# Next pair's matrices and merge ahead of a pair's head scaling; out-projection, norms and feed-forward one turn later

## What is computed

```python
# x: [8, 256, 256]; H, DK, DV = 6, 32, 64
q, k, v = (silu(causal_conv4(x @ W.T, w)) for W, w in ...)      # depthwise, 4 taps
beta = sigmoid(x @ Wb.T);  g = -exp(A_log) * softplus(x @ Wa.T + dt_bias)
q = l2norm(q) * DK ** -0.5;  k = l2norm(k)
def step(S, (qt, kt, vt, gt, bt)):                              # per batch and head, over 256 tokens
    S = S * exp(gt)
    S = S + bt * outer(kt, vt - kt @ S)
    return S, qt @ S
o = scan(step, S0=0)
o = o * rsqrt(mean(o * o, -1) + 1e-5) * norm_w * silu(x @ Wg.T) # gating, per head
x = layernorm(x + o @ Wo.T)
xq = ternary_quantize(x, 0.33, 0.5);  w = ternary_quantize(weight, 0.2, 0.6) + rram_variation
x = layernorm(x + xq @ w.T)
```

## Time and profile before

| | |
|---|---|
| median of 3 runs | 350.73 us (350.22 to 351.06) |
| the profiled execution: its time | 353.02 us |
| its span | 351.2 us |
| TensorE matmuls busy | 252.8 us, 72% |
| VectorE busy | 268.5 us, 76% |
| ScalarE busy | 146.8 us, 42% |
| chain that ended last | TensorE 53%, VectorE 22%, issue 18%, ScalarE 5% |

### The profile page before, as it was taken

The page is one execution under the profiler, slowest core; times in us unless marked ns, Lnnn a source line. Parts: engine busy times, 40 slices in busy tenths (PEclk is TensorE's granted clock), DMA queues, the critical chain, the costliest instruction groups (busy, mean ns, idle before and its releaser), DMA issues.

```text
span 351.2 us, 15117 instructions
## 1 busy us (share of the span) xinstructions
PE 252.8 (72%) x6956; PEld 178.0 (51%) x6956; DVE 268.5 (76%) x660; ACT 146.8 (42%) x271; POOL 9.2 (3%) x14
## 2 busy tenths in 40 slices
PE   2978943986479958958699589776928458967571
PEld 1435421666455535756455356665607357755441
DVE  0688999563999995969999887589999960546966
ACT  1497763255463602734636214635423024024031
POOL 2110000001000000010000000100000000000000
PEclk9999976698989985999989955999876757969898
DMA  7900000000000002000001020000010002000101
GB/s 231 359 0 2 3 1 0 4 4 6 4 5 4 0 0 63 6 4 6 6 4 60 0 63 4 4 7 4 4 60 0 2 5 63 6 5 4 60 1 60
DMA packets 8031, 9.82 MB, mean 28 GB/s; under 512 B 1568, under 2 KB 7072, under 8 KB 7968
## 3 DMA queue, kind: packets, MB, share of 16 engines
q1 hardware_dynamic: 6480, 8.39, 7.2%
q10 hardware_dynamic: 1488, 0.47, 0.5%
HBM read 6.76 MB, written 2.10 MB: 25 GB/s over the span
## 4 chain that ended last, share of the span: by engine, by line
PE 53%; DVE 22%; issue 18%; ACT 5%; DMA 1%; DVEq 0%; SPq 0%; ACTq 0%
PE fr L322 15%; PE pj L335 10%; PE pj L350 5%; PE pg L322 5%; PE pc L322 4%; DVE conv_buf L958 4%; PE po L322 3%; PE pc L479 3%; PE po L479 2%; PE pj L509 2%; DMA xt<-x_t 1%; PE pj L367 1%; DVE tok_buf L970 1%; DVE ss L991 1%; DVE stats L1222 1%
## 5 line engine op out<-in xcount | busy, mean ns | idle before, releaser
L335 PE MATMUL pj<-xt,wproj 128*128 128x512 f32 x96 | 53.6, 706 | 8.4 <-DMA xt<-x_t 6.4
L958 DVE SCALAR_TENSOR_TENSOR conv_buf<-raw,wconv,conv_buf 128x512 f32<-128x512 f32 x72 | 53.3, 755 | 4.9 <-ACT conv_buf L663 3.2
L335 PEld LDWEIGHTS pj<-xt,wproj 128*128 128x128 f32 x96 | 20.0, 220 | 31.0 <-issue 24.0
L662 ACT ACTIVATE raw<-pj 128x512 f32<-128x512 f32 x24 | 14.3, 596 | 34.7 <-PE pj L335 34.7
L1088 DVE TENSOR_TENSOR mq<-fr,ad 128x512 f32<-128x512 f32 x12 | 8.3, 692 | 26.5 <-PE fr L322 26.5
L350 PE MATMUL pj<-xt,wproj 128*128 128x512 f32 x48 | 25.1, 664 | 4.6 <-ACT conv_buf L663 4.6
L322 PE MATMUL fr<-x_t,x 32*32 32x16 f32 x768 | 11.5, 209 | 21.6 <-issue 21.6
L322 PEld LDWEIGHTS fr<-x_t,x 32*32 32x32 f32 x768 | 10.9, 151 | 24.3 <-issue 24.3
L322 PE MATMUL fr<-kga,wu 32*32 32x64 f32 x768 | 14.7, 228 | 7.2 <-issue 7.2
L350 PEld LDWEIGHTS pj<-xt,wproj 128*128 128x128 f32 x48 | 10.0, 213 | 16.4 <-issue 8.4
L727 ACT ACTIVATE s_sb<-po 128x192 f32<-128x192 f32 x12 | 4.0, 330 | 32.8 <-PE po L322 32.8
(11 more groups left out here) (181 smaller groups left out, 578.2 us busy)
## 6 DMA issues: line engine op xcount, KB each, us to landing
xt<-x_t SPq DMA_DIRECT2D x1, 1536.0 KB, 11.4
res<-x SPq DMA_DIRECT2D x3, 512.0 KB, 4.1
out<-hid_buf SPq DMA_DIRECT2D x6, 256.0 KB, 2.1
wproj<-w_proj SPq DMA_DIRECT2D x1, 1024.0 KB, 7.4
xt<-x_t SPq DMA_DIRECT2D x1, 512.0 KB, 5.0
kq<-x SPq DMA_DIRECT2D x1, 512.0 KB, 3.8
wout<-w_out SPq DMA_DIRECT2D x1, 384.0 KB, 11.7
cst<-consts ACTq DMA_DIRECT2D x1, 305.5 KB, 11.4
```

The lines of the kernel that those rows point to most:

```text
L335: mm = pe.matmul(pj[:, j % 2, :], wproj[:, t, j * P:(j + 1) * P], xt[:, t, k * TOK:(k + 1) * TOK], start=(t == 0), stop=(t == KT - 1))
L662: act.activation(raw[:, j, :, TAPS - 1:], bank, ACT.Copy)
L958: e = dve.scalar_tensor_tensor(out=conv[:, d, :, :], in0=raw[:, d, :, m:m + T], scalar=wconv[:, j, m:m + 1], in1=conv[:, d, :, :], op0=ALU ...
```

## The change

On VectorE the head work of a pair is split in two: `head_factors` (sums, root) stays ahead of the next pair's `chunk_matrices`, `head_scale` (scaling and transposes) goes behind `inverse_to_rows`, and `gated` goes into the next turn, behind `inverse`, which is now first in the turn. `attention_sum`, `first_norm` and `ternary` of pair k - 1 move behind the first three conv tiles; `transition_sum` is gone. On TensorE each transition block begins with a product of the identity with `ad`, and ScalarE copies the sum out (`transition_out`). `project_out(k - 1)` stands between the transition blocks of turn k and writes `pj`; `gates(k)` are in turn k instead of k - 1, in turn 3 inside the recurrence and into `fr`; `ternary_turned` is at chunk 5, `feed_forward` at chunks 6 and 7. ScalarE's order follows. `ternary` writes into `hid_buf` instead of `tok_buf`, and the token transpose loses a wait. The heads of the last pair are finished inside the last turn, the first half ahead of the feed-forward sums and the second behind them.

```diff
-        pos = view(tok_buf, 0, TT, HID, dt=BF16)
-        xq = view(tok_buf, TT * HID // 2, TT, HID, dt=BF16)
+        pos = view(hid_buf, 0, TT, HID, dt=BF16)
+        xq = view(hid_buf, TT * HID // 2, TT, HID, dt=BF16)
...
+        a_bank = (pj[:, 0, :], pj[:, 1, :])
...
                 if first(k):
                     pe.wait_ge(ffn_ready, 2)
                 after(pe, tile_out, CONV_TILES, k, CONV_TILES)
-                if not first(k):
-                    after(pe, gate_done, 0, k, GATE_TILES)
-                    after(pe, ffn_in, 0, k - 1, 2)
+                if k > 1:
+                    after(pe, ffn_in, 2, k - 2, 2)
                 for n in range(2):
                     pe.matmul(pj[:, n, 0:UH * CH].rearrange("p (u t) -> p u t", t=CH), identb[:, :],
                               negb[:, :].unsqueeze(1).to_broadcast([P, UH, CH]), start=True, stop=False)
...
                 if b == 0:
                     after(pe, kg_done, 1, k, 1)
                     after(pe, at_done, 1, k, 1)
+                    after(pe, decay_in, 1, k, 1)
+                    after(pe, qe_done, 1, k, 1)
+                pe.matmul(fr[:, b, :], cst[:, C_IDENT:C_IDENT + P],
+                          ad[:, :, :, :].rearrange("p c g x -> p (c g x)")[:, b * MB * 64:(b + 1) * MB * 64],
+                          start=True, stop=False, skip_group_check=True)
                 for n in range(b * MB, (b + 1) * MB):
                     i = n - b * MB
                     mm = by_head(fr[:, b, i * 64:(i + 1) * 64], wu[:, n, 0:DK], kga[:, k % 2, n // G3, n % G3, :],
-                                 start=True, stop=True)
+                                 start=False, stop=True, skip_group_check=True)
                 mm.then_inc(mq_mm, 1)
 
             def new_state(k, c):
...
                 merge_second(k)
                 if front:
                     project(k + 1, 5)
-                solved(k, 0)
-                solved(k, 1)
-                if not first(k):
-                    ternary_turned(k - 1)
-                for b in range(2, 5):
+                for b in range(5):
                     solved(k, b)
                 new_state(k, 0)
                 heads_out(k, 0)
                 new_state(k, 1)
                 for b in range(3):
                     transitions(k, b)
-                    if not front and b < 2:
-                        feed_forward(k - 1, b)
+                    if not first(k) and b < 2:
+                        project_out(k - 1, b)
                 for c in range(1, NC):
                     carried_state(k, c)
                     if c < NC - 2:
                         new_state(k, c + 1)
                     heads_out(k, c)
-                    if front and not first(k) and c in (2, 3):
-                        feed_forward(k - 1, c - 2)
+                    if not front and c <= GATE_TILES:
+                        gates(k, c - 1)
+                    if not first(k) and c == NC - 3:
+                        ternary_turned(k - 1)
+                    if not first(k) and c >= NC - 2:
+                        feed_forward(k - 1, c - (NC - 2))
                 if front:
-                    exponents(k + 1)
                     for g in range(G3):
                         chunk_products(k + 1, g)
+                    exponents(k + 1)
                     if not last(k + 1):
                         for j in range(4):
                             project(k + 2, j)
-                    gates(k + 1, 0)
-                    gates(k + 1, 1)
-                    project_out(k, 0)
-                    project_out(k, 1)
-                    gates(k + 1, 2)
+                    for j in range(GATE_TILES):
+                        gates(k, j)
                     merge(k + 1)
                     if not last(k + 1):
                         project(k + 2, 4)
...
                 act.activation(wu[:, b * WB:b * WB + n, :].rearrange("p u x -> p (u x)"), wu_bank[b][:, 0:n * 96],
                                ACT.Copy).then_inc(wu_out, 1)
 
+            def transition_out(k, b):
+                after(act, mq_mm, b + 1, k, 3)
+                act.activation(mq[:, b * MB:(b + 1) * MB, :].rearrange("p u x -> p (u x)"), fr[:, b, :],
+                               ACT.Copy).then_inc(mq_in, 1)
+
             def state_out(k, c):
                 after(act, s_mm, c + 1, k, NC - 1)
                 act.activation(s_sb[:, (c + 1) % 2, :], s_bank[c % 2][:, 0:G3 * DV], ACT.Copy).then_inc(s_done, 1)
...
                     weight_part(1)
                 if front:
                     tile_out_of_psum(k + 1, 4)
-                if not first(k):
-                    normalize(k - 1, 0)
-                if front:
                     tile_out_of_psum(k + 1, 5)
-                solved_out(k, 0)
-                solved_out(k, 1)
-                if not first(k):
-                    ternary_out(k - 1)
-                for b in range(2, 5):
+                for b in range(5):
                     solved_out(k, b)
                 if first(k):
                     weight_part(2)
                 state_out(k, 0)
                 if front:
-                    for j in range(3):
-                        silu(k + 1, j)
+                    silu(k + 1, 0)
+                transition_out(k, 0)
+                if front:
+                    silu(k + 1, 1)
+                transition_out(k, 1)
+                transition_out(k, 2)
+                if front:
+                    silu(k + 1, 2)
                 for c in range(1, NC):
                     if c < NC - 1:
                         state_out(k, c)
                     if c % 2:
                         heads_out(k, c // 2)
-                    if not front:
-                        if c % 2:
+                        if not front:
                             heads_square(k, c // 2)
-                        continue
-                    if c == 1:
+                    if not front and c <= GATE_TILES:
+                        gate_silu(k, c - 1)
+                    if not first(k) and c == 3:
+                        normalize(k - 1, 0)
+                    if front and c == 4:
                         square(k + 1)
-                    if 3 <= c < 6:
-                        silu(k + 1, c)
-                    if c >= 5:
-                        heads_square(k, c - 5)
-                    if c == NC - 1:
-                        heads_square(k, 3)
+                    if front and c == 5:
+                        silu(k + 1, 3)
+                    if not first(k) and c == NC - 2:
+                        ternary_out(k - 1)
                 if front:
+                    for j in range(4, CONV_TILES):
+                        silu(k + 1, j)
+                    for n in range(NC // 2):
+                        heads_square(k, n)
                     exp_d(k + 1)
                     if not last(k + 1):
                         for j in range(4):
...
                 after(dve, silu_done, 3, k, CONV_TILES)
-                if k > 1:
-                    after(dve, xqt_mm, 0, k - 1, 1)
...
                     return v.rearrange("p (g c) -> p g c", g=G3).unsqueeze(3).to_broadcast([P, G3, NC, DK])
+                if not first(k):
+                    after(dve, mq_mm, 3, k - 1, 3)
                 dve.tensor_tensor(by_group(kr[:, :, :, 0:DK]), kq_tok[:, :, 0, :, :], rows(fk[:, :]),
                                   ALU.mult).then_inc(kc_done, 1)
                 dve.tensor_tensor(qe_tok.rearrange("p (g c) d -> p g c d", g=G3), kq_tok[:, :, 1, :, :],
...
                 else:
                     rsqrt(r_all[:, :], v_all[:, :], t_all[:, :])
                     shifts()
+
+            def head_scale(k):
                 units = o_all[:, :, :, :].rearrange("p g c v -> p (g c) v")
                 dve.tensor_tensor(units, units, r_o.unsqueeze(2).to_broadcast([P, U, DV]),
                                   ALU.mult).then_inc(on_scaled, 1)
...
                     dve.scalar_tensor_tensor(out=o_half, in0=o_half, scalar=nw[:, j:j + 1], in1=g_half,
                                              op0=ALU.mult, op1=ALU.mult).then_inc(end_gated, 1)
 
+            def end_heads(s):
+                end_head_sums(s)
+                rsqrt(head_r[s], head_v[s], t_all[:, 0:UF])
+                end_head_scale(s)
+                end_to_channels(s)
+                end_gate(s)
+
             def end_factors(bank, s):
 
                 pair = slice(2 * s, 2 * s + 2)
...
 
             def turn(k, front):
                 head_eps(k)
+                inverse(k)
                 if first(k):
-                    conv_taps(1, 0)
                     ffn_weights(2)
                 else:
+                    gated(k - 1)
+                if front:
+                    for j in range(3):
+                        conv_taps(k + 1, j)
+                if not first(k):
                     attention_sum(k - 1, 0)
                     attention_sum(k - 1, 1)
                     first_norm(k - 1)
```

(30 more changed lines are left out.)

64 lines of the change are left out of this document (23 added, 41 removed).

## The result

The changed kernel takes **370.22 us** (median; 369.27 to 370.53) against 350.48 for the kernel before on the same chip: ratio 1.0585, 95% interval 1.0545 to 1.0626, 19.7 us slower. The profiled execution took 370.03 us with a span of 368.1, 17.0 over the profiled execution before; that one lay 0.65% over its median, so traces are compared by the 17 and medians by the 19.7.

A forecast was written before the change was run, and what follows sets the result against it. VectorE was taken to bound the middle turns and TensorE's chain turn 3. Terms -0.5 + 4.0 + 4.0 + 8.5 + 4.9 gave +20.9 us: 373.9 against the profiled 353.0, 371.5 against the median 350.7; range 360 to 382.

The forecast's parts named there:

- Turn 0: First turn: identity products and ScalarE delay the token transpose 4.6, head scaling and gating leave (-7.1), squares and clock add: -0.5 us.
- Turns 1 and 2: Middle turns: VectorE waits for the out-projection between transition blocks before its attention sums: +4.0 us each.
- the start of the stretch: Turn 1: VectorE's unbroken work after t_t starts at 159.7 instead of 155.6, 4.1 us later; turn 2 likewise +4.1.
- 0.55 shorter: Turns 1 and 2, VectorE's unbroken work: 7.1 us leaves; second attention sum, first norm and ternary come in.
- ScalarE's queue, 0 to 3, I take 0.5: Turns 1 and 2: tile 2's activation and the first normalization ahead of chunk-state copies delay recurrence and ternary: +0.5 us.
- The 1 us for the clock: Turn 0: TensorE idles longer before the first merge, so a slower solve may follow: 0 to 3.5 us, 1 taken.
- Turn 3's transitions: TensorE in turn 3: identity products and out-projection come in, feed-forward halves and ternary transposes leave, some gaps fill: +4.0 us.
- Recurrence: TensorE in turn 3: 7.2 us of new matmuls cost 0.55 of their length, +4.0 us, plus 0.5 for ScalarE.
- The end: After turn 3's recurrence: feed-forward's second half, its sum and moments, root and shift precede the second head sums: +4.9 us.
- slower, turn 3's transitions at half clock: Rival: TensorE's low clock lasts through turn 3's transitions, products and identities cost 8.1 us once more: 380 us, chance 0.15.
- The gaps take the added matmuls: Rival, less slow: gaps between TensorE's small matmuls absorb the added ones: +11.7 us, 362 us, chance 0.2.
- Faster: Rival: VectorE's new waits are met in time if the second product comes some 9 us after t_t: 345 us, chance 0.05.

The follow-up runs named there:

- the run with a third of the projection: The changed kernel with only one of three channel tiles in the out-projection of pairs 0 to 2: 358.51 us, ratio 1.0241.
- the run with the early last turn: The changed kernel with ScalarE's first normalization, TensorE's ternary transposes and feed-forward halves at earlier chunks in turn 3 alone: 367.02 us, ratio 1.0495.

## Why the prediction was right

The time (371.5 against 370.2), the side and the mechanism came out: VectorE's wait for the transitions was replaced by a longer one for the out-projection behind them, and turn 3 is longer. The terms were less good than their sum. Turn 0 and the recurrence of turn 3 came out 4.2 and 2.9 us below their terms, turns 1 and 2 and the end 3.5 above; that the sum lies so near is in part luck.

- **Turns 1 and 2**: +4.0 each predicted, +4.9 each measured. In turn 1 the start of the stretch gave +3.1 of the +4.1; the run with a third of the projection shows it as the cause. "0.55 shorter" failed: it is 0.7 longer, 1.3 of it the collision with GpSimd, which the prediction did not look at. The merge at its end was 1.1 longer, with a gap of 1.66 in its second product where before has none (the clock was at 0.50 ahead of it in both). In turn 2 the start gave only +1.5, and the stretch is 3.2 longer: GpSimd again, and 2.4 us of waiting for the normalization, of which "ScalarE's queue, 0 to 3, I take 0.5" took too little. In turn 1 the ternary did not wait; in turn 2 the clock was at 0.50 from 238 to 243, in the recurrence that stands ahead of the normalization.
- **Turn 0**: -0.5 predicted, -4.7 measured. The length is -7.1 to the tenth; the start, from t_t, is +2.5, not +4.6. The step that failed is "three identity products (2.9) delay the transitions": without them the transpose comes 0.5 earlier, since they fill gaps. The prediction let gaps take up matmuls in turns 1 to 3 and not here. The transitions took 7.2 us with the products and 6.9 before without them: before had 1.5 us more of gaps and ran at clock 0.52 from 82.0 to 85.5. The 1 us for the squares did not occur. The 1 us for the clock did, as 1.7: at 0.51 from 70.4 to 73.9 the project tile ahead of the solve took 3.66 us in place of 1.98; a gap of 1.16 us that the solve had before, and 0.15 after, takes most of it back.
- **Turn 3's transitions**: +4.0, measured +3.2.
- **Recurrence**: "7.2 x 0.55 = +4.0" and 0.5 for ScalarE, measured +1.6. That this is near the low end of 1.3 is chance. The new matmuls took 7.7 and the 5.9 us of gaps were all filled, as at that low end; the wait for the other engines was 2.0 (1.8 of it ScalarE's) and not 0.5; and 2.2 came off because before's recurrence ran from 310.7 to 317.5 at clock 0.50, which the prediction did not see. At one clock the recurrence is 3.1 to 3.9 us longer, near the 4.5, with another split. What the prediction quotes beside this sum, that fetching instructions is mostly hidden and the gaps would be something else, does not hold in these stretches: the gaps are waits for instructions, and longer matmuls do fill them.
- **The end**: +4.9, measured +6.6. The prediction took feed-forward as what comes last; it was ready at 334.0 and VectorE busy to 335.05 with the first heads, late through a normalization at chunk 3. The run with the early last turn takes 3.8 of it back.
- **The scaling**: the sum was 3.9 too high against the profiled execution. The profile of after lay at its median and that of before 2.5 above, so the step "353.0 to 350.7" hid 2.6 of it: against the median the forecast is 1.3 too high. The time is nearer than the sum was.
- **Rivals**: "slower, turn 3's transitions at half clock" did not come: the clock was at 0.50 in the solve, 0.89 from 298 to 303 and 1.00 from 303 on. "The gaps take the added matmuls" was right about the gaps, in turn 3 and in turn 0, and wrong for the total, since ScalarE's order and the end gave more than it allowed. (Its +2.5 for each of turns 1 and 2 is 2.8 with the gap of 1.45 filled whole.) "Faster" was off by its own condition: the second product came 16.4 us after t_t, not 9.

## What to carry to other kernels

Before a consumer is moved, ask what stands ahead of its producer on the other engine, and for whom the producer's engine is the chain: here a product done in spare time was moved into the one stretch that VectorE waits for. Try a change's parts apart: the smallest one, a sum moved from VectorE to products and a copy, is worth 10 us alone (with three taps moved ahead of a transpose), and was buried under what is by subtraction 30 us of the rest. And when a wait is mended, work out which one stands behind it; mending five places at once brought 6 us of the 15 to 27 hoped for. Before a stretch of two traces is compared, compare its clock: here 2.2 us of a recurrence were the clock's, more than the difference that was read.

## What the hardware showed unexpectedly

- A VectorE operation on 128x4 took 1.48 us in place of 0.16 beside a GpSimd product of 1.48 us, and 0.16 again when that product ran in idle time. Beside the token transpose of turn 0, which has one input in place of two, the same product did no harm.
- TensorE waits for its own instructions where matmuls are small. In before 31 gaps of 0.3 to 2.1 us, 39.6 us in all, lie multiples of 256 matmuls and weight loads apart (within two), and each ends 1.2 to 1.6 us after a transfer of 16,384 bytes on the instruction queue has ended. In the four recurrences of before, of 17 to 19 us, they are 3.2 to 7.7 us.
- Longer matmuls fill these gaps: in after 7.7 us of new ones left none of the 5.9 us of gaps, and at clock 1.00 the recurrence is 3.1 to 3.9 us longer, 2.0 of it waits for the other engines.
- A move on VectorE alone changed when such a transfer came on TensorE, and the clock behind it, and the kernel was 1.3% (0.5 to 2.1%) slower. Why the transfer came later is open.
